# Count stage of a graph kernel: two-input compares, 128-column operands, and PSUM accumulators grouped in pairs

## The chip, the cores and the metric

The kernel runs on one core of a Trainium2 chip, as one launch. The metric is device time in microseconds (us) of a whole launch, lower is better. Three runs of the kernel before gave 2707.4, 2709.84 and 5465.59 us; their median is 2709.84 us. The profiled execution took 2711.62 us.

## The reference

Four graph layers in a row (a three-layer single-head GAT, a two-layer GCN, a relational GAT with four heads, an attention layer with FFN) work on one graph of 3125 nodes and 103,125 edges, 128 features per node, each followed by a residual and a layer norm. All of them use the edges only through sums over edges grouped by destination:

```
edge_index = jnp.stack([src, dst])                      # dst is sorted, edge_type_3 is 0, 1 or 2
out = jax.ops.segment_sum(msg, dst, num_segments=N)     # messages of edges added per destination
mask = jnp.concatenate([edge_type == r, jnp.ones((N,), dtype=bool)])   # third layer: relation r, and self loops
x = _layernorm(x + layer(x, edges, weights))            # four times
```

## The kernel before

The kernel first turns the edge list into dense count matrices, how many edges go from source s to destination d, for each of the three relations (`counts`) and in all (`counts_all`), and all layers then multiply by these. This case is about the stage that makes them, `count_edges`; the rest of the kernel is as it was.

**Tiling.** The 3125 nodes are 25 rows of P = 125. A destination is one of NG = 625 groups of DG = 5 destinations. The loop over i (25 iterations) takes 125 destinations, that is 25 groups b. A group's counts are a 125 x 375 matrix: source within its row by (relation, source row, destination within the group), 3 x 25 x 5 = 375 columns (GW; GE is 376, one more to keep it even). `prepare` has gathered, for every group, a window of WIN = 2 chunks of 125 edges that holds all edges of the group, one edge per partition: `window_lo` (source within its row) and `window_col` (column).

**One group.** DVE makes one-hot matrices by comparing an iota with these keys. For `lo1` (128 wide, both chunks, 1280 elements per partition) it does five groups in one compare of two tensors, L334. For `col1` (376 wide) it makes one compare with a per-partition scalar for each chunk, L339, ten for five groups. PE multiplies them, two matmuls of 375 columns added in one PSUM bank (L384). ACT copies the bank, 125 x 375, to the f16 tile `stage` (L438), where a group's columns become 75 runs of 5 elements: the destination is the innermost dimension of a row of 128.

**Sums over relations.** After each group b of `ADDED` = (3, 8, 13, 18, 23), PE adds the three relations of 25 destinations that are already in `stage` with six identity matmuls into two more banks (`add_up`, L370, called "the sums" below): sums number n = 0 after b = 3 (for the last 25 destinations of the iteration before), n = 1 after b = 8, and so on. Sums n wait (L367) until ACT has moved the result of sums n - 1 out of these two banks. ACT moves it to the tile `total` with two instructions (`move_total`, L427), which stand in its program after the copy of group b + 1, that is after b = 4, 9, 14, 19 and 24.

**What orders it.** The engines run their own programs in order and meet in counting semaphores: `hot` (one-hots of a group ready), `counted` (a group's matmuls done), `taken` (a group copied to `stage`), `summed` and `moved` (sums made, moved). Five banks hold groups (bank b % 5), two the sums. DVE may be at most five groups ahead of PE. POOL adds the self loops to `stage` and `total` (L322, four instructions per iteration, once the next iteration's n = 0 is moved), then the SP queue stores both, four DMAs of 800 KB (L453, L455). `stage` has three slots, `total` two. The branch for edges that do not fit the windows (`v.Else`, `pe.Else`) is not taken here.

Of the kernel before, what the change touches and what calls it, by code (L numbers as in the profile page):

```python
# [11 lines left out]
F32 = mybir.dt.float32  # L12
# [57 lines left out]
def prepare(nc, K, S):  # L70
# [7 lines left out]
    with ExitStack() as ctx:  # L78
# [20 lines left out]
        si = sb("si", [P, NG], I32)  # L99
        order = sb("order", [P, NG], F16)  # L100
        ki = sb("ki", [P, GE], I32)
        pi = sb("pi", [P, PAD, 2], I32)
        wt = sb("wt", [D, 6, D], F32)
        a = sb("a", [D, 6, 8], F32)
        m = sb("relm", [128, 2], F32)
# [6 lines left out]
        with nc.Block() as block:  # L112
# [27 lines left out]
            @block.gpsimd  # L140
            def _(pool):
                pool.iota(si[:], [[1, P], [P, DG]], channel_multiplier=0).then_inc(iotas, 1)
                pool.memset(K.ident[:], 0.0).then_inc(cleared, 1)
                pool.memset(K.ident16[:], 0.0).then_inc(cleared, 1)
                pool.memset(K.zeros[:], 0.0).then_inc(made, 1)
                pool.wait_ge(cleared, 2)
                for mat in (K.ident, K.ident16):
                    pool.affine_select(out=mat[:], in_=mat[:], compare_op=ALU.not_equal, fill=1.0, base=0,
                                       pattern=[[-1, 128]], channel_multiplier=1).then_inc(made, 1)
                pool.iota(gi[:], [[P, DG]], channel_multiplier=1).then_inc(iotas, 1)  # L150
                pool.iota(ti[:], [[GW, NG]], channel_multiplier=0).then_inc(iotas, 1)
                pool.iota(ki[:], [[1, GE]], channel_multiplier=0).then_inc(iotas, 1)
                pool.iota(pi[:], [[1, PAD], [0, 2]], channel_multiplier=0).then_inc(iotas, 1)
# [137 lines left out]
def count_edges(nc, K, S):  # L291
# [7 lines left out]
    STEPS = NCH // SLOTS  # L299
    HALVES = ((0, 13), (13, NB))  # L300
    ADDED = (3, 8, 13, 18, 23)

    with ExitStack() as ctx:
        sb = lambda name, shape, dt: ctx.enter_context(nc.sbuf_tensor(name, shape, dt))
        lo1 = sb("lo1", [P, P // DG, PAD, WIN], BF16)
        col1 = sb("col1", [P, SLOTS, GE], BF16)
        stage, total = K.stage, K.total
        lo_wide = lo1[:].rearrange("p s l w -> p (s l w)")[:, 0:SLOTS * PAD].rearrange("p (s l) -> p s l", l=PAD)
        (hot, counted, taken, summed, stored, diag, wide_hot, wide_used, moved) = (
# [2 lines left out]
        with nc.Block() as block:  # L312
# [12 lines left out]
            def _(v):  # L325
                wide = v.value_load(K.wide[0:1, 0:1], min_val=0, max_val=1)
                with v.If(wide < 1):
                    with v.Fori(0, NB) as i:
                        for b in range(P // DG):

                            v.wait_ge(counted, i * (P // DG) + b + 1)
                            if b % OHS == 0:

                                v.tensor_tensor(  # L334
                                    lo1[:, b:b + OHS], K.iota_pair[:].unsqueeze(1).to_broadcast([P, OHS, PAD, WIN]),
                                    K.window_lo[:, bass.ds(i * (P // DG) + b, OHS)].unsqueeze(2)
                                    .to_broadcast([P, OHS, PAD, WIN]), ALU.is_equal)
# [19 lines left out]

            @block.tensor
            def _(pe):
                pe.sem_inc(counted, OHS)  # L360
                pe.sem_inc(moved, 1)
                def add_up(i, n, own=True):

                    slot, q = (i % STAGES, n - 1) if own else ((i + STAGES - 1) % STAGES, 4)
                    pe.wait_ge(taken, i * (P // DG) + 5 * n + OHS)

                    pe.wait_ge(moved, 5 * i + n + 1)  # L367
                    for half, (h0, h1) in enumerate(HALVES):
                        for r in range(R):
                            ins = pe.matmul(K.ps[0:P, OHS + half, 0:(h1 - h0) * NB], K.ident16[0:P, 0:P],  # L370
                                            stage[0:P, bass.ds(slot, 1), r, h0:h1, bass.ds(25 * q, 25)]
                                            .rearrange("p a h d -> p (a h) d"), start=(r == 0), stop=(r == R - 1))
                    ins.then_inc(summed, 1)

                wide = pe.value_load(K.wide[0:1, 0:1], min_val=0, max_val=1)
                with pe.If(wide < 1):
                    with pe.Fori(0, NB) as i:
                        for b in range(P // DG):
                            s = b % OHS
                            pe.wait_ge(hot, i * (P // DG) + b + 1)  # L380
# [8 lines left out]
                with pe.Else():  # L389
                    pe.sem_inc(wide_used, 1)  # L390

                    def five_groups(i):
                        for s in range(OHS):

                            pe.wait_ge(taken, i * OHS + s + 1)
                            pe.matmul(K.ps[:, s, :], K.zeros[0:P, 0:128], K.zeros[0:P], start=True, stop=True)
                            with pe.Fori(0, STEPS) as c:
                                pe.wait_ge(wide_hot, i * (OHS * STEPS) + s * STEPS + c + 1)
                                for w in range(SLOTS):
                                    ins = pe.matmul(K.ps[0:P, s, 0:GW], lo_wide[:, w, 0:P], col1[:, w, 0:GW],  # L400
                                                    start=False, stop=False, skip_group_check=True)
                                ins.then_inc(wide_used, 1)

                            pe.matmul(K.ps[:, s, 0:128], K.zeros[0:P, 0:128], K.zeros[0:P, 0:128], start=False, stop=False,
                                      skip_group_check=True).then_inc(counted, 1)

                    with pe.Fori(0, NB) as i:
                        add_up(i, 0, own=False)
                        with pe.Fori(0, 4) as q:
                            five_groups(i * 5 + q)  # L410
                            add_up(i, q + 1)
                        five_groups(i * 5 + 4)

                add_up(NB, 0, own=False)

            @block.scalar
            def _(act):
                act.sem_inc(taken, OHS)

                def move_total(i, n):  # L420
                    act.wait_ge(summed, 5 * i + n + 1)
# [2 lines left out]
                        act.wait_ge(stored, 64 * i + 64 * (STAGES - 1))  # L424
                    slot, q = (i % 2, n - 1) if n else ((i + 1) % 2, 4)
                    for half, (h0, h1) in enumerate(HALVES):
                        ins = act.activation(total[0:P, bass.ds(slot, 1), h0:h1, 25 * q:25 * q + 25]  # L427
                                             .rearrange("p a h d -> p (a h) d"),
                                             K.ps[0:P, OHS + half, 0:(h1 - h0) * NB].rearrange("p (h d) -> p h d", d=NB),
                                             ACT.Copy)  # L430
                    ins.then_inc(moved, 1)

                with act.Fori(0, NB) as i:
                    act.wait_ge(stored, 64 * i + 64)
                    for b in range(P // DG):
                        act.wait_ge(counted, i * (P // DG) + b + 1 + OHS)
                        dst = stage[0:P, bass.ds(i % STAGES, 1), :, :, DG * b:DG * (b + 1)]
                        act.activation(dst.rearrange("p a r h d -> p (a r h) d"),  # L438
                                       K.ps[0:P, b % OHS, 0:GW].rearrange("p (x d) -> p x d", d=DG),
                                       ACT.Copy).then_inc(taken, 1)  # L440
# [1037 lines left out]
def build(nc, args, out):  # L1478
# [5 lines left out]
    with ExitStack() as ctx:  # L1484
# [25 lines left out]
        with nc.cleanup_on_exit():  # L1510
            with ExitStack() as c2:
# [4 lines left out]
                K.iota_pair = sb2("iota_pair", [P, PAD, WIN], F16)  # L1516
# [159 lines left out]
```

## Time and profile before

| | us |
|---|---|
| median of three runs | 2709.84 |
| profiled execution | 2711.62 |
| its span, first to last instruction | 2709.8 |
| count stage, first compare to last move of a total | 58.4 to 463.2 |
| one iteration of the stage, from the fourth on | 15.7 |

Of the whole span PE is busy 78%, DVE 79%, ACT 69%, POOL 3%. These are means over many stages. The count stage is some 405 us of it, and its numbers are read from windows inside it. In an answer of the trace on the order of time a row gives start and length in us, engine, line, operation, tiles and shapes and the number of merged instructions, and in brackets how long the engine had been idle before it and what ended that. Instructions of one engine overlap a little, so what an engine needs for one is the distance from start to start and not the duration; a length of n merged ones is n - 1 distances and one duration.

### The profile page before, as it was taken

The numbers are of one execution on the slowest core, as the hardware profiler recorded it, in microseconds if no ns is written. First come the engines' busy times: TensorE is split into PE (matmuls) and PEld (weight loads), VectorE is DVE, ScalarE is ACT, GpSimd is POOL, SyncE is SP. The second block draws the span as 40 slices with busy tenths as digits, with TensorE's granted clock in tenths as the row PEclk, the third lists the DMA queues.
The fourth block names the chain that finished last, engine by engine and source line by source line (L and its number), as shares of the span: only waits on it lengthen the run. The fifth ranks groups of instructions, "written<-read, shape, count | busy, mean of one in ns | idle before, by whom it ended". The sixth has DMA issues, their size and how long they took to land. (4 is left out here: it accounts for less than half of the span.)

```text
span 2709.8 us, 90541 instructions
## 1 busy us (share of the span) xinstructions
PE 2126.6 (78%) x34148; PEld 1879.1 (69%) x34148; DVE 2149.4 (79%) x4334; ACT 1869.8 (69%) x3038; POOL 85.4 (3%) x137
## 2 busy tenths in 40 slices
PE   3999997698599699494957999489995898766636
PEld 3655554598598598493957899389994898756624
DVE  6999997688787788606068999799988999949963
ACT  5999997666766765302049999599987999645522
POOL 1111111000000000000000000000000000000000
PEclk8999998799799799697988899799997999878868
DMA  3355455342342342171723331233303333034100
GB/s 100 147 224 210 193 220 216 108 143 78 99 152 77 108 143 77 61 242 61 242 72 92 92 105 52 81 95 107 102 28 110 98 95 107 3 110 133 60 0 24
DMA packets 182326, 302.60 MB, mean 112 GB/s; under 512 B 6476, under 2 KB 158927, under 8 KB 182058
## 3 DMA queue, kind: packets, MB, share of 16 engines
q1 hardware_dynamic: 181273, 297.57, 33.4%
q8 instruction: 208, 3.41, 0.6%
q0 software_dynamic: 800, 1.26, 0.2%
q14 instruction: 45, 0.37, 0.0%
HBM read 214.26 MB, written 84.54 MB: 110 GB/s over the span
## 5 line engine op out<-in xcount | busy, mean ns | idle before, releaser
L438 ACT ACTIVATE stage<-ps 125x375 f32 x625 | 314.0, 603 | 39.3 <-PE ps L384 34.9
L339 DVE TENSOR_SCALAR col<-iota_col,window_col 125x376 bf16<-125x376 f16 x1250 | 311.4, 327 | 4.4 <-PE ps L384 4.4
L384 PE MATMUL ps<-col,lo 125*125 125x375 bf16 x1250 | 290.9, 345 | 17.8 <-DVE col L339 17.5
L1007 ACT ACTIVATE r1amsk<-r1ad,r1thr 125x640 f16 x360 | 260.0, 815 | 2.5 <-DVE r1asel L1029 2.4
L1007 ACT ACTIVATE r2amsk<-r2ad,r2thr 125x640 f16 x360 | 259.7, 817 | 0.1
L1007 ACT ACTIVATE r0amsk<-r0ad,r0thr 125x640 f16 x360 | 259.6, 814 | 0.1
L1080 PE MATMUL ps<-r1mv,r1asel 125*128 125x66 f16 x5000 | 243.8, 196 | 9.8 <-issue 8.5
L1080 PE MATMUL ps<-r2mv,r2asel 125*128 125x66 f16 x5000 | 243.0, 196 | 5.3 <-issue 4.8
L1080 PE MATMUL ps<-r0mv,r0asel 125*128 125x66 f16 x5000 | 244.7, 197 | 0.3 <-DVE r0asel L1029 0.3
L384 PEld LDWEIGHTS ps<-col,lo 125*125 125x125 bf16 x1250 | 137.0, 139 | 145.0 <-DVE col L339 142.0
L1080 PEld LDWEIGHTS ps<-r1mv,r1asel 125*128 125x128 f16 x5000 | 227.0, 100 | 13.9 <-issue 9.1
L1080 PEld LDWEIGHTS ps<-r2mv,r2asel 125*128 125x128 f16 x5000 | 227.1, 100 | 7.9 <-issue 5.1
L1080 PEld LDWEIGHTS ps<-r0mv,r0asel 125*128 125x128 f16 x5000 | 229.2, 100 | 2.0 <-DVE r0asel L1029 0.4
L1084 PE MATMUL ps<-r0mv,r0ct 125*128 125x132 f16 x1250 | 181.2, 229 | 5.4 <-issue 5.4
L1084 PE MATMUL ps<-r1mv,r1ct 125*128 125x132 f16 x1250 | 180.3, 228 | 0.0
L1084 PE MATMUL ps<-r2mv,r2ct 125*128 125x132 f16 x1250 | 180.2, 228 | 0.0
L1225 PE MATMUL ps<-parts,ct 125*128 125x128 f16 x2500 | 150.4, 222 | 36.1 <-DVEq L1234 33.3
L1225 PEld LDWEIGHTS ps<-parts,ct 125*128 125x128 f16 x2500 | 143.2, 99 | 43.3 <-DVEq L1234 33.7
L949 PE MATMUL ps<-g0mv,g0asel 125*128 125x130 f16 x2500 | 147.9, 220 | 0.0
L949 PE MATMUL ps<-g2mv,g2asel 125*128 125x130 f16 x2500 | 147.3, 220 | 0.0
L949 PE MATMUL ps<-g1mv,g1asel 125*128 125x130 f16 x2500 | 147.0, 219 | 0.0
L949 PEld LDWEIGHTS ps<-g0mv,g0asel 125*128 125x128 f16 x2500 | 145.7, 97 | 0.6
(540 smaller groups left out, 4500.2 us busy)
## 6 DMA issues: line engine op xcount, KB each, us to landing
counts<-stage SPq DMA_DIRECT2D x75, 800.0 KB, 4.8
ct<-counts_all SPq DMA_DIRECT2D x75, 800.0 KB, 4.7
counts_all<-total SPq DMA_DIRECT2D x25, 800.0 KB, 7.3
g0ct<-counts_all SPq DMA_DIRECT2D x25, 800.0 KB, 4.6
g1ct<-counts_all SPq DMA_DIRECT2D x25, 800.0 KB, 4.7
g2ct<-counts_all SPq DMA_DIRECT2D x25, 800.0 KB, 4.6
r0ct<-counts SPq DMA_DIRECT2D x25, 800.0 KB, 4.7
r1ct<-counts SPq DMA_DIRECT2D x25, 800.0 KB, 6.3
```

The source lines that it names most:

```text
L339: ins = v.tensor_scalar(col1[:, b % OHS * WIN + w], K.iota_col[:], K.window_col[:, bass.ds(i * (P // DG) + b, 1), w], None, ALU.is_equal)
L384: ins = pe.matmul(K.ps[0:P, s, 0:GW], lo1[:, b, 0:P, w], col1[:, s * WIN + w, 0:GW], start=(w == 0), stop=(w == WIN - 1))
L438: act.activation(dst.rearrange("p a r h d -> p (a r h) d"), K.ps[0:P, b % OHS, 0:GW].rearrange("p (x d) -> p x d", d=DG), ACT.Copy).then_i ...
L949: ins = pe.matmul(K.ps[:, b, a * F:(a + 1) * F], sel[:, s % 5, a, b], T.mv[:, s, (2 * p + a) * F:(2 * p + a + 1) * F], start=False, stop=F ...
L1007: act.activation(msk[:, s % 5, n], ad[:, bass.ds(g % 2, 1), h] .rearrange("p a (b d) -> p (a b) d", d=PAD), ACT.Sigmoid, bias=T.thr[:, 1, ...
L1080: pe.matmul(K.ps[:, b, 2 * h * F:2 * (h + 1) * F], sel[:, s % 5, h, b], vs[:, (h * 2 + p) * 2 * F:(h * 2 + p + 1) * 2 * F], start=False, s ...
L1084: ins = pe.matmul(K.ps[:, b, 0:2 * HF].rearrange("p (h a f) -> p h a f", h=H, a=2)[:, :, 1], ct[0:P, s // 5, b, s % 5], vs[:, (4 + p) * HF ...
L1225: ins = pe.matmul(K.ps[:, b, 0:D], ct[0:P, s // 5, b, s % 5], parts[:, s, p], start=(s == 0 and p == 0), stop=(s == NB - 1 and p == 1))
```

## The change

- **Column one-hots.** They are made like `lo1`, by a compare of two tensors, for two groups and then for three, both chunks at once, into `col2`: [3 buffers, 5 groups, 376, 2 chunks], chunk innermost. So the matmul reads its moving operand with a step of two elements. `window_col` is f16 instead of f32 for that, `iota_pair` is 376 long instead of 128, and DVE waits once per five groups.
- **128 columns.** The stationary operands of L384 and L370 are 128 wide instead of 125, and so are the PSUM outputs and the copies.
- **Pairs.** Groups are taken in 13 pairs p (the last is group 24 alone). A pair has two neighbouring banks of six, in turns of three; the sums have banks 6 and 7. ACT copies a pair with one instruction of 2 x 375. PE waits for a free pair of banks before each pair's first group.
- **Place of the moves.** `move_total` stands after pairs 2, 5, 7, 10 and 12 for n = 0 to 4, so after the copy of groups 5, 11, 15, 21 and 24. `ADDED` is as it was.

```diff
-        pi = sb("pi", [P, PAD, 2], I32)
+        pi = sb("pi", [P, GE, 2], I32)
...
+    GROUPS = P // DG
+    SUMS = 6
+    PAIRS = [(b, min(b + 2, GROUPS)) for b in range(0, GROUPS, 2)]
+    BANK = [2 * (p % 3) for p in range(12)] + [2]
+    MOVED = {2: 0, 5: 1, 7: 2, 10: 3, 12: 4}
+    LAST = [max(p for p in range(len(PAIRS)) if BANK[p] == bank) for bank in (0, 2, 4)]
...
-        col1 = sb("col1", [P, SLOTS, GE], BF16)
+        col1 = sb("col1", [P, 30, GE], BF16)
+        col2 = col1[:].rearrange("p s c -> p (s c)").rearrange("p (a s c w) -> p a s c w", a=3, s=OHS, w=WIN)
...
-                        for b in range(P // DG):
-                            v.wait_ge(counted, i * (P // DG) + b + 1)
-                            if b % OHS == 0:
-                                v.tensor_tensor(
-                                    lo1[:, b:b + OHS], K.iota_pair[:].unsqueeze(1).to_broadcast([P, OHS, PAD, WIN]),
...
-                            for w in range(WIN):
-                                ins = v.tensor_scalar(
-                                    col1[:, b % OHS * WIN + w], K.iota_col[:],
-                                    K.window_col[:, bass.ds(i * (P // DG) + b, 1), w], None, ALU.is_equal)
-                            ins.then_inc(hot, 1)
+                        for n in range(GROUPS // OHS):
+                            v.wait_ge(counted, i * GROUPS + (5, 10, 10, 15, 20)[n])
+                            v.tensor_tensor(
+                                lo1[:, OHS * n:OHS * n + OHS], K.iota_pair[:, 0:PAD].unsqueeze(1).to_broadcast([P, OHS, PAD, WIN]),
...
+                            for s0, s1 in ((0, 2), (2, OHS)):
+                                v.tensor_tensor(
+                                    col2[:, n % 3, s0:s1], K.iota_pair[:].unsqueeze(1).to_broadcast([P, s1 - s0, GE, WIN]),
+                                    K.window_col[:, bass.ds(i * GROUPS + OHS * n + s0, s1 - s0)].unsqueeze(2)
+                                    .to_broadcast([P, s1 - s0, GE, WIN]), ALU.is_equal).then_inc(hot, s1 - s0)
...
+                def bank_free(i, b):
+                    p = b // 2
+                    earlier = [q for q in range(p) if BANK[q] == BANK[p]]
+                    if earlier:
+                        pe.wait_ge(taken, i * GROUPS + PAIRS[earlier[-1]][1] + GROUPS)
+                    else:
+                        pe.wait_ge(taken, i * GROUPS + PAIRS[LAST[BANK[p] // 2]][1])
...
-                            pe.wait_ge(taken, i * (P // DG) + b + 1)
+                            if b % 2 == 0:
+                                bank_free(i, b)
                             for w in range(WIN):
-                                ins = pe.matmul(K.ps[0:P, s, 0:GW], lo1[:, b, 0:P, w], col1[:, s * WIN + w, 0:GW],
+                                ins = pe.matmul(K.ps[:, BANK[b // 2] + b % 2, 0:GW], lo1[:, b, :, w],
+                                                col2[:, b // OHS % 3, b % OHS, 0:GW, w],
...
-                    for b in range(P // DG):
-                        act.wait_ge(counted, i * (P // DG) + b + 1 + OHS)
-                        dst = stage[0:P, bass.ds(i % STAGES, 1), :, :, DG * b:DG * (b + 1)]
...
-                        if b - 1 in ADDED:
-                            move_total(i, ADDED.index(b - 1))
+                    for p, (b0, b1) in enumerate(PAIRS):
+                        act.wait_ge(counted, i * GROUPS + b1 + 2 * OHS)
+                        dst = stage[:, bass.ds(i % STAGES, 1), :, :, DG * b0:DG * b1]
+                        act.activation(dst.rearrange("p a r h (s d) -> p s (a r h) d", d=DG),
+                                       K.ps[:, BANK[p]:BANK[p] + b1 - b0, 0:GW].rearrange("p s (x d) -> p s x d", d=DG),
+                                       ACT.Copy).then_inc(taken, b1 - b0)
+                        if p in MOVED:
+                            move_total(i, MOVED[p])
...
-                K.window_col = sb2("window_col", [P, NG, WIN], F32)
+                K.window_col = sb2("window_col", [P, NG, WIN], F16)
```

## Rows read from the trace of the kernel before

**Rows 1.** Busy time by window, one iteration: PE, PEld, DVE, ACT, POOL, clock, DMA
```profile
251.38:267.09 15.71, 15.18 (x82) 9.11 (x81) 15.71 (x57) 14.95 (x36) 2.10 (x4) 1.00 0.51 209
```
**Rows 2.** Who waited for whom, 62 to 455 us: total, times, longest
```profile
PEld ps L384 <- DVE col L339: 136.1, 456, 0.6
ACT stage L438 <- PE ps L384: 16.2, 26, 1.4
PE ps L370 <- ACT total L427: 4.3, 8, 2.6
```
**Rows 3.** Timeline of DVE from 267 us: compares of five groups
```profile
267.09 0.82 DVE L334 TENSOR_TENSOR lo<-iota_pair,window_lo 125x1280 bf16<-125x1280 f16 x1
267.82 2.36 DVE L339 TENSOR_SCALAR col<-iota_col,window_col 125x376 bf16<-125x376 f16 x10
```
**Rows 4.** Timeline from 257 us, POOL beside DVE
```profile
257.58 1.71 POOL L322 TENSOR_TENSOR stage<-stage,ident 125x125 f16 x3 [13.60 <-ACT total L427]
258.12 3.04 DVE L339 TENSOR_SCALAR col<-iota_col,window_col 125x376 bf16<-125x376 f16 x10
```
**Rows 5.** Timeline from 109 us, where PE was not held by DVE
```profile
108.69 1.75 PE L384 MATMUL ps<-col,lo 125*125 125x375 bf16 x10
109.29 0.67 ACT L438 ACTIVATE stage<-ps 125x375 f32 x1 [1.26 <-PE ps L384]
109.80 0.74 ACT L427 ACTIVATE total<-ps 125x325 f32 x2
110.68 1.04 PE L370 MATMUL ps<-stage,ident 125*125 x6 [0.24 <-ACT total L427]
111.56 1.16 PE L384 MATMUL ps<-col,lo 125*125 125x375 bf16 x5
```
**Rows 6.** Timeline of ACT from 263 us, instruction by instruction
```profile
263.10 0.44 ACT L427 ACTIVATE total<-ps 125x325 f32 x1
263.43 0.41 ACT L427 ACTIVATE total<-ps 125x300 f32 x1
263.73 0.51 ACT L438 ACTIVATE stage<-ps 125x375 f32 x1
264.10 0.52 ACT L438 ACTIVATE stage<-ps 125x375 f32 x1
264.48 0.70 ACT L438 ACTIVATE stage<-ps 125x375 f32 x1
264.97 0.54 ACT L438 ACTIVATE stage<-ps 125x375 f32 x1
```
**Rows 7.** Groups of instructions, 0 to 62 us (second number after the first bar: mean ns)
```profile
L258 ACT ACTIVATE stage<-zeros 128x28800 f16<-128x28800 bf16 x1 | 24.2, 24204 | 9.2 <-POOL zeros L145 9.2
L258 ACT ACTIVATE total<-zeros 128x6400 f16<-128x6400 bf16 x1 | 5.5, 5519 | 0.0
```
**Rows 8.** Busy time by window, the third iteration
```profile
89.27:110.06 20.79, 17.16 (x81) 11.65 (x80) 16.74 (x57) 14.60 (x34) 4.12 (x8) 0.84 0.76 310
```
**Rows 9.** Timeline from 101 us, in the third iteration
```profile
101.53 0.77 ACT L427 ACTIVATE total<-ps 125x325 f32 x2 [3.38 <-DMA counts_all<-total]
102.44 0.53 PE L370 MATMUL ps<-stage,ident 125*125 x1 [2.58 <-ACT total L427]
```
**Rows 10.** Groups of instructions, whole span
```profile
L1080 PEld LDWEIGHTS ps<-r0mv,r0asel 125*128 125x128 f16 x5000 | 229.2, 100 | 2.0 <-DVE r0asel L1029 0.4
L384 PEld LDWEIGHTS ps<-col,lo 125*125 125x125 bf16 x1250 | 137.0, 139 | 145.0 <-DVE col L339 142.0
L370 PEld LDWEIGHTS ps<-stage,ident 125*125 125x125 f16 x756 | 99.1, 136 | 27.4 <-issue 15.6
L917 DVE TENSOR_TENSOR g1asel<-g1ct,g1asel 125x640 f16<-125x640 f16 x125 | 61.5, 492 | 4.3
```
**Rows 11.** Timeline of the preparation, the instructions that grow
```profile
33.78 0.29 DVE L198 CAST iota_pair<-pi 125x256 f16<-125x256 int32 x1
37.24 1.53 POOL L158 DMA_INDIRECT above<-edge_keys,rows_of  x1 [22.05 <-DVE rows_of L210]
```

More of the change, by code:

```diff
@@ L152, in _ @@
                 pool.iota(ki[:], [[1, GE]], channel_multiplier=0).then_inc(iotas, 1)
-                pool.iota(pi[:], [[1, PAD], [0, 2]], channel_multiplier=0).then_inc(iotas, 1)
+                pool.iota(pi[:], [[1, GE], [0, 2]], channel_multiplier=0).then_inc(iotas, 1)
                 pool.wait_ge(rows_ready, 1)
@@ L328, in _ @@
                     with v.Fori(0, NB) as i:
[L329 to L342 removed]
+                        for n in range(GROUPS // OHS):
+                            v.wait_ge(counted, i * GROUPS + (5, 10, 10, 15, 20)[n])
+                            v.tensor_tensor(
+                                lo1[:, OHS * n:OHS * n + OHS], K.iota_pair[:, 0:PAD].unsqueeze(1).to_broadcast([P, OHS, PAD, WIN]),
+                                K.window_lo[:, bass.ds(i * GROUPS + OHS * n, OHS)].unsqueeze(2)
+                                .to_broadcast([P, OHS, PAD, WIN]), ALU.is_equal)
+                            for s0, s1 in ((0, 2), (2, OHS)):
+                                v.tensor_tensor(
+                                    col2[:, n % 3, s0:s1], K.iota_pair[:].unsqueeze(1).to_broadcast([P, s1 - s0, GE, WIN]),
+                                    K.window_col[:, bass.ds(i * GROUPS + OHS * n + s0, s1 - s0)].unsqueeze(2)
+                                    .to_broadcast([P, s1 - s0, GE, WIN]), ALU.is_equal).then_inc(hot, s1 - s0)
                 with v.Else():
@@ L359, in _ @@
             def _(pe):
-                pe.sem_inc(counted, OHS)
+                pe.sem_inc(counted, 2 * OHS)
                 pe.sem_inc(moved, 1)
+                def bank_free(i, b):
[5 more added lines that the diff above has]
+                        pe.wait_ge(taken, i * GROUPS + PAIRS[LAST[BANK[p] // 2]][1])
                 def add_up(i, n, own=True):
                     slot, q = (i % STAGES, n - 1) if own else ((i + STAGES - 1) % STAGES, 4)
-                    pe.wait_ge(taken, i * (P // DG) + 5 * n + OHS)
+                    pe.wait_ge(taken, i * GROUPS + 5 * n + GROUPS)
                     pe.wait_ge(moved, 5 * i + n + 1)
@@ L369, in add_up @@
                         for r in range(R):
-                            ins = pe.matmul(K.ps[0:P, OHS + half, 0:(h1 - h0) * NB], K.ident16[0:P, 0:P],
-                                            stage[0:P, bass.ds(slot, 1), r, h0:h1, bass.ds(25 * q, 25)]
+                            ins = pe.matmul(K.ps[:, SUMS + half, 0:(h1 - h0) * NB], K.ident16[:],
+                                            stage[:, bass.ds(slot, 1), r, h0:h1, bass.ds(25 * q, 25)]
                                             .rearrange("p a h d -> p (a h) d"), start=(r == 0), stop=(r == R - 1))
@@ L377, in _ @@
                     with pe.Fori(0, NB) as i:
-                        for b in range(P // DG):
-                            s = b % OHS
-                            pe.wait_ge(hot, i * (P // DG) + b + 1)
-                            pe.wait_ge(taken, i * (P // DG) + b + 1)
+                        for b in range(GROUPS):
+                            pe.wait_ge(hot, i * GROUPS + b + 1)
+                            if b % 2 == 0:
+                                bank_free(i, b)
                             for w in range(WIN):
-                                ins = pe.matmul(K.ps[0:P, s, 0:GW], lo1[:, b, 0:P, w], col1[:, s * WIN + w, 0:GW],
+                                ins = pe.matmul(K.ps[:, BANK[b // 2] + b % 2, 0:GW], lo1[:, b, :, w],
+                                                col2[:, b // OHS % 3, b % OHS, 0:GW, w],
                                                 start=(w == 0), stop=(w == WIN - 1))
@@ L390, in _ @@
                     pe.sem_inc(wide_used, 1)
[L392 to L405, printed above, removed]
@@ L407, in _, with one_group @@
-                    with pe.Fori(0, NB) as i:
[L408 to L412, printed above, removed]
+                    def one_group(i, b):
+                        bank = BANK[b // 2] + b % 2
+                        bank_free(i, b)
+                        pe.matmul(K.ps[:, bank, :], K.zeros[0:P, 0:128], K.zeros[0:P], start=True, stop=True)
+                        with pe.Fori(0, STEPS) as c:
+                            pe.wait_ge(wide_hot, i * (GROUPS * STEPS) + b * STEPS + c + 1)
+                            for w in range(SLOTS):
+                                ins = pe.matmul(K.ps[:, bank, 0:GW], lo_wide[:, w], col1[:, w, 0:GW],
+                                                start=False, stop=False, skip_group_check=True)
+                            ins.then_inc(wide_used, 1)
+                        pe.matmul(K.ps[:, bank, 0:128], K.zeros[0:P, 0:128], K.zeros[0:P, 0:128], start=False, stop=False,
+                                  skip_group_check=True).then_inc(counted, 1)
@@ L414, in _ @@
+                    with pe.Fori(0, NB) as i:
+                        for b in range(GROUPS):
+                            one_group(i, b)
+                            if b in ADDED:
+                                add_up(i, ADDED.index(b), own=(b != ADDED[0]))
                 add_up(NB, 0, own=False)
@@ L417, in _ @@
             def _(act):
-                act.sem_inc(taken, OHS)
+                act.sem_inc(taken, GROUPS)
                 def move_total(i, n):
@@ L426, in move_total @@
                     for half, (h0, h1) in enumerate(HALVES):
-                        ins = act.activation(total[0:P, bass.ds(slot, 1), h0:h1, 25 * q:25 * q + 25]
+                        ins = act.activation(total[:, bass.ds(slot, 1), h0:h1, 25 * q:25 * q + 25]
                                              .rearrange("p a h d -> p (a h) d"),
-                                             K.ps[0:P, OHS + half, 0:(h1 - h0) * NB].rearrange("p (h d) -> p h d", d=NB),
+                                             K.ps[:, SUMS + half, 0:(h1 - h0) * NB].rearrange("p (h d) -> p h d", d=NB),
                                              ACT.Copy)
@@ L434, in _ @@
                     act.wait_ge(stored, 64 * i + 64)
-                    for b in range(P // DG):
-                        act.wait_ge(counted, i * (P // DG) + b + 1 + OHS)
-                        dst = stage[0:P, bass.ds(i % STAGES, 1), :, :, DG * b:DG * (b + 1)]
-                        act.activation(dst.rearrange("p a r h d -> p (a r h) d"),
-                                       K.ps[0:P, b % OHS, 0:GW].rearrange("p (x d) -> p x d", d=DG),
-                                       ACT.Copy).then_inc(taken, 1)
-                        if b - 1 in ADDED:
-                            move_total(i, ADDED.index(b - 1))
+                    for p, (b0, b1) in enumerate(PAIRS):
[6 more added lines that the diff above has]
+                            move_total(i, MOVED[p])
                 move_total(NB, 0)
@@ L1515, in build @@
                 K.iota_col = sb2("iota_col", [P, GE], F16)
-                K.iota_pair = sb2("iota_pair", [P, PAD, WIN], F16)
+                K.iota_pair = sb2("iota_pair", [P, GE, WIN], F16)
                 K.window_lo = sb2("window_lo", [P, NG, WIN], F16)
-                K.window_col = sb2("window_col", [P, NG, WIN], F32)
+                K.window_col = sb2("window_col", [P, NG, WIN], F16)
                 K.wide = sb2("wide", [1, 1], I32)
```

## The prediction

> **What bounds the stage now.** I read first the busy time of single iterations, then the waits, then the timeline. An iteration takes 15.71 us and DVE is busy for all of it [rows 1]; PE waited for `col` 456 times [rows 2], with 625 groups in the whole stage. So DVE sets the pace. ACT is close behind, 14.95 us busy. Five groups cost DVE 0.73 us for `lo` (start to start) and 2.27 for the ten column compares, 3.00 in all [rows 3]. Once per iteration POOL's four additions come between: the ten compares then last 3.04 instead of 2.36, +0.68 [rows 4]. 5 x 3.00 + 0.68 = 15.7, the measured period.
>
> PE alone would be faster: matmuls start every 0.16 us ((1.75 - 0.32) / 9, with 0.32 for the last one's own duration), six sums hold it 1.04 at most, 0.84 without the start-up [rows 5]. 50 x 0.16 + 5 x 0.84 = 12.2 us. What it does when DVE doesn't hold it is seen once, and the prediction rests on it [rows 5]. The copy of the group begun at 108.69 starts 0.60 later (two matmuls 0.48, then 0.13 until ACT is off); the total is moved by 110.54; 0.14 later the sums start, and PE had idled 0.24. That is the loop sums, copy, move of a total, next sums. It is hidden today because four groups lie between the copy that precedes the move and the next sums, and at DVE's pace these take 4 x 0.45.
>
> **DVE's part.** `lo` has 1280 elements, lasts 0.82 and costs 0.73 start to start [rows 3]; one of the same kind with 640 lasts 0.49 [rows 10]. So 0.33 / 640 = 0.52 ns per element, and 0.07 fixed. The new compares have the same kind, dtypes and broadcast: 2 x 752 elements 0.85, 3 x 752 elements 1.24. Five groups: 0.73 + 0.85 + 1.24 = 2.82. With POOL's four interruptions, which I leave at 0.68 (they already wait for a two-input compare at 257.58, rows 4), an iteration would be 14.8 us: -0.9, if DVE stayed the bound.
>
> **ACT's part.** A copy of 375 costs 0.37 to 0.38 or 0.49 start to start [rows 6]. Which one goes by group. The 75 runs of 5 f16 start at byte 10b of their row; the four copies shown are groups 15 to 18, and the long one is 17, whose run, bytes 170 to 180, crosses a multiple of 16. So do 12 of the 25. A pair has the same runs, so its cost is the two singles less one fixed part. From the two fills, (24204 - 5519) / 22400 = 0.834 ns per element [rows 7]; 375 elements are 0.313, so the fixed part of a start-to-start 0.375 is 0.06. A pair with one long copy: 0.375 + 0.495 - 0.06 = 0.81. Ends: 0.87 (nothing saved) and 0.63 (750 elements at 0.834 and nothing else). The Trainium skill (ScalarE: Activation LUTs, What ACT_TABLE_LOAD costs) has back-to-back ACTIVATEs at a fixed 93 ns beyond the elements; by it the pair is 0.78 and the period below 0.2 us shorter, and the sum doesn't use it. Moving a total stays 0.33 + 0.41 = 0.74 [rows 6].
>
> **The new order, on the path.** Sums n still wait for total n - 1 to be moved. That move now stands after groups 5, 11, 15, 21, 24 instead of 4, 9, 14, 19, 24. Before sums 1, 2, 3, 4, 0 PE has only 3, 2, 3, 2, 4 groups left to do, and ACT copies a pair only when its second group is done. From the start of one set of sums to the start of the next, with 0.88 for the sums after a wait (110.68 to 111.56, rows 5), 0.32 per full group, 0.48 for a last one, 0.13 to ACT and 0.13 back:
> - 1 to 2: group 9 must end before pair (8, 9) is copied, then pair (10, 11), then the total: 0.88 + 0.48 + 0.13 + 0.81 + 0.81 + 0.74 + 0.13 = 3.98. PE's own work there is 0.84 + 10 x 0.16 = 2.4, so it idles 1.5.
> - 2 to 3: pair (14, 15) needs two groups after the sums: 0.88 + 0.32 + 0.48 + 0.13 + 0.81 + 0.74 + 0.13 = 3.49.
> - 3 to 4, as the first: 3.98.
> - 4 to 0: group 24 alone is copied, 0.88 + 0.48 + 0.13 + 0.51 + 0.13 = 2.13; only then are the banks free for pair (2, 3), since the last pair uses the same ones; two groups and the start-up, 0.70. 2.83.
> - 0 to 1: pair (4, 5), as 2 to 3 less the start-up, 3.45.
>
> Sum 17.7 us per iteration, against DVE's 14.8, ACT's own 13.3 (13 x 0.375 + 12 x 0.495 - 12 x 0.06 + 5 x 0.62) and PE's 12.2: nobody is full, they take turns. With a pair at 0.87 it is 18.1, at 0.63 16.6 (six pairs are on the loop).
>
> So (17.73 - 15.71) x 25 = +51. Against it, the third iteration loses less. Today ACT waits 3.38 us in it for the first store of a total and PE stops for 2.6 [rows 9]; the iteration has a mean clock of 0.84, so a third of it at 1.2 GHz, and takes 20.8 us, 5 more than the others [rows 8]. At 17.7 us per iteration that move comes at about 102, when the store has landed: -5. Sum +46. Later stores have room, the DMA engines are busy 0.51 x 15.7 = 8 us per iteration [rows 1]. At the ends +55 and +19.
>
> **At nothing.** The stationary loads should fall from 139 towards 100 ns [rows 10], but they lie under matmuls of 160. POOL's iota is three times as long under a wait of 22 us. The cast of `iota_pair` (0.29) grows by some 0.3 us beside sums that PE still has to finish [rows 11], the first group's one-hots come 0.4 later; if no cover holds, +0.7 in all. POOL's additions each wait for a longer compare, up to 4.4 us instead of 2.1; the store that follows has that slack, without it the total's double buffer would hold ACT.
>
> **Forecast.** 2711.6 + 46 = 2758 in the profiled execution, 2756 against the median of 2709.84, since that execution was 1.8 above it. Its own range is 2729 to 2767. 2%, about what a measurement of this kernel tells from no change, is 54 us: 2764. Chance 0.63, of which 0.17 above 2764.
>
> **Rivals.**
> - DVE stays the bound: I misread the loop, or ACT is much quicker with a pair. 14.8 us, 25 x -0.9 = -22: 2688. For it: ACT was busy 14.95 of 15.71 and sheds twelve fixed parts. Against: the loop falls to 15.7 only if a pair costs 0.46, below its elements' 0.63. Decides from there on. 0.20, of which 0.03 faster by over 2%.
> - The moving operand reads at half rate. Today 375 neighbouring bf16 take 0.16, which is 2.4 GHz with one column per cycle; with every second element, twice the bytes are passed over. No row shows a moving operand with a step; a stationary one with the same step (`lo`) loads in 139 ns beside 136 without [rows 10], which speaks against. Matmuls at 0.31: the segments become 4.75, 4.13, 4.75, 4.0, 4.13, sum 21.8, +6.1 x 25 - 5: 2859. The Trainium skill, SBUF — State Buffer, gives this port 2 bytes per lane and cycle (A bandwidth-pool intuition that's wrong), which would do this, but also says (Door 1) that two hits per 16-byte line give full rate, which a step of 4 bytes has. No run shows either. 0.10.
> - The wide compares fall to one element per cycle, twice the 0.52 ns: 3760 x 1.04 ns + 0.13 + 0.73 = 4.78 per five groups, 24.6 per iteration, 2930. Against: `lo` has the same form. 0.03.
> - PE's clock falls in the idle stretches. It is at 1.00 over whole iterations [rows 1] and fell only in the iteration with the stop of 2.6 us [rows 8, 9]; here PE would stop 1.5 us at most and work 60% of its idlest segment. At half clock throughout, matmuls as in the rival above and sums longer too, up to 2950. 0.04.
>
> **Sum of chances.** Faster by over 2%: 0.03. Slower by over 2%: 0.17 + 0.10 + 0.03 + 0.04 = 0.34. Within: 0.63. The range takes the forecast's 2729 to 2767 and reaches down to the first rival: 2686 to 2773.
>
> **What would show it.** Right: iterations of 17.7 us; DVE idle about 3 us in each, ended by L384; PE idle 1.5 before the second and fourth sums and 1 before the first and third, ended by ACT's total; a pair's copy about 0.81 start to start; matmuls still 0.16 apart. Wrong: DVE busy throughout, matmuls 0.31 apart, column compares of 1.6 and 2.4 us, a clock below 1.00 in the stage, or a pair far from 0.81.

## The result, and the profile after

The changed kernel takes 2762.55 us, median of four runs (2755.81 to 2769.8), beside 2708.62 for the kernel before in the same comparison: ratio 1.020, 95% interval 1.019 to 1.021. One of the four runs of the kernel before took 5465.59 us, twice its usual time; without it that median is 2707.4. The changed kernel's profiled execution is the quickest of its four, 2755.81, with a span of 2754.0 and a mean clock of 0.904.

One steady iteration of the stage by the window view (columns as in [rows 1]):

```profile
270.13:288.35 18.22, 13.50 (x82) 7.39 (x80) 15.25 (x16) 14.71 (x24) 4.39 (x5) 1.00 0.44 180
```

18.22 us, against 15.71 in [rows 1]. No engine fills it: DVE was busy for all of its iteration before and now lacks 3 us, and ACT's busy time has hardly moved. The clock stays at 1.00. The waits from 62 to 500 us, which are most of the stage, to be held against [rows 2]:

```profile
PE ps L385 <- ACT total L441: 111.6, 95, 1.4
ACT stage L452 <- PE ps L399: 104.9, 121, 19.6
DVE lo L339 <- PE ps L399: 75.3, 47, 4.2
PE ps L399 <- DVE col L344: 5.3, 1, 5.3
```

PE waited for `col` 456 times; now once. Its new wait is for the move of a total, 95 times in the 119 sums of that window, and ACT waits for PE nearly as long. One iteration of PE by the timeline, five sums and the matmuls between them:

```profile
273.95 1.01 PE L385 MATMUL ps<-stage,ident 128*128 x6 [1.40 <-ACT total L441]
274.82 1.82 PE L399 MATMUL ps<-col,lo 125*128 125x375 bf16 x10
277.57 1.00 PE L385 MATMUL ps<-stage,ident 128*128 x6 [0.93 <-ACT total L441]
...
281.65 1.00 PE L385 MATMUL ps<-stage,ident 128*128 x6 [1.42 <-ACT total L441]
...
284.46 1.00 PE L385 MATMUL ps<-stage,ident 128*128 x6
...
288.11 1.00 PE L385 MATMUL ps<-stage,ident 128*128 x6 [0.98 <-ACT total L441]
```

The idle times alternate, 1.4 and 0.95. The same stretch on ACT shows why: two pair copies stand ahead of the total where PE waits 1.4, one where it waits 0.95.

```profile
271.35 1.86 ACT L452 ACTIVATE stage<-ps 128x750 f32 x2 [0.77 <-PE ps L399]
273.05 0.76 ACT L441 ACTIVATE total<-ps 128x325 f32 x2
...
275.77 1.02 ACT L452 ACTIVATE stage<-ps 128x750 f32 x1 [1.08 <-PE ps L399]
276.68 0.75 ACT L441 ACTIVATE total<-ps 128x325 f32 x2
```

Taken one by one, the two copies of the first row are:

```profile
271.35 1.02 ACT L452 ACTIVATE stage<-ps 128x750 f32 x1 [0.77 <-PE ps L399]
272.21 1.00 ACT L452 ACTIVATE stage<-ps 128x750 f32 x1
```

And DVE, which stops twice per iteration because PE is behind:

```profile
275.08 2.17 DVE L344 TENSOR_TENSOR col<-iota_pair,window_col 125x1504 bf16<-125x1504 f16 x2
279.06 0.83 DVE L339 TENSOR_TENSOR lo<-iota_pair,window_lo 125x1280 bf16<-125x1280 f16 x1 [1.81 <-PE ps L399]
279.80 2.18 DVE L344 TENSOR_TENSOR col<-iota_pair,window_col 125x1504 bf16<-125x1504 f16 x2
283.14 0.82 DVE L339 TENSOR_TENSOR lo<-iota_pair,window_lo 125x1280 bf16<-125x1280 f16 x1 [1.16 <-PE ps L399]
```

The first compare comes at 60.09 (before 58.38) and the last move of a total ends at 525.62 (463.15): the stage is 60.8 us longer. The profiled execution is only 44 longer, because everything behind the stage took 18 us less than in the profiled execution of before. The stages of the third layer show it, before (first fence) and after (second), by the window view:

```profile
1399.10:1722.40 323.30, 264.31 (x6339) 256.91 (x6339) 294.61 (x359) 290.11 (x411) 3.14 (x2) 0.90 0.29 86
1722.40:2045.50 323.10, 264.43 (x6339) 255.09 (x6340) 290.12 (x355) 290.54 (x411) 3.16 (x3) 0.90 0.30 86
```

```profile
1460.35:1778.08 317.73, 263.64 (x6339) 255.66 (x6339) 294.27 (x359) 290.12 (x411) 3.14 (x2) 0.90 0.30 88
1778.08:2094.72 316.64, 262.00 (x6339) 254.49 (x6339) 289.97 (x355) 290.04 (x411) 3.14 (x2) 0.92 0.29 88
```

The same instructions with the same busy times on DVE and ACT, 6 us shorter each. The profiled executions of experiments 1, 3, 6 and 9 below give back 10 to 18 us behind the stage too, that of experiment 2 nothing. The granted clock differs in one of the two windows only. Over everything behind the stage it is 0.89 against 0.88, so part of the 18 us may be the clock; but in experiment 6 it is 0.88 there as before, and that part is 10 us shorter all the same. Why stays open.

### The profile page after: what moved, and what is told of

Its sections match the earlier page's. It is cut to its first block and busy times, and to the rows that moved or that the text cites. A ratio compares the mean times of both kernels' runs of the same rounds, so it can differ in the third digit from the quotient of the medians.

```text
span 2754.0 us, 86841 instructions
## 1 busy us (share of the span) xinstructions
PE 2082.4 (76%) x34148; PEld 1826.1 (66%) x34148; DVE 2135.2 (78%) x3334; ACT 1863.3 (68%) x2738; POOL 145.2 (5%) x137
## 5 line engine op out<-in xcount | busy, mean ns | idle before, releaser
L452 ACT ACTIVATE stage<-ps 128x750 f32 (+1 forms) x325 | 306.0, 982 | 109.1 <-PE ps L399 109.1
L344 DVE TENSOR_TENSOR col<-iota_pair,window_col 125x1504 bf16<-125x1504 f16 x250 | 281.7, 1167 | 0.0
L399 PE MATMUL ps<-col,lo 125*128 125x375 bf16 x1250 | 235.3, 330 | 5.4 <-DVE col L344 5.3
L385 PE MATMUL ps<-stage,ident 128*128 x756 | 128.0, 305 | 121.0 <-ACT total L441 117.8
L385 PEld LDWEIGHTS ps<-stage,ident 128*128 128x128 f16 x756 | 72.7, 96 | 188.8 <-issue 168.4
L399 PEld LDWEIGHTS ps<-col,lo 125*128 125x128 bf16 x1250 | 113.8, 97 | 92.7 <-issue 16.7
L339 DVE TENSOR_TENSOR lo<-iota_pair,window_lo 125x1280 bf16<-125x1280 f16 x125 | 112.1, 897 | 78.1 <-PE ps L399 76.5
```

The lines of the kernel that those rows point to most:

```text
L339: v.tensor_tensor(lo1[:, OHS * n:OHS * n + OHS], K.iota_pair[:, 0:PAD].unsqueeze(1).to_broadcast([P, OHS, PAD, WIN]), K.window_lo[:, bass. ...
L344: v.tensor_tensor(col2[:, n % 3, s0:s1], K.iota_pair[:].unsqueeze(1).to_broadcast([P, s1 - s0, GE, WIN]), K.window_col[:, bass.ds(i * GROU ...
L385: ins = pe.matmul(K.ps[:, SUMS + half, 0:(h1 - h0) * NB], K.ident16[:], stage[:, bass.ds(slot, 1), r, h0:h1, bass.ds(25 * q, 25)] .rearran ...
L399: ins = pe.matmul(K.ps[:, BANK[b // 2] + b % 2, 0:GW], lo1[:, b, :, w], col2[:, b // OHS % 3, b % OHS, 0:GW, w], start=(w == 0), stop=(w = ...
L452: act.activation(dst.rearrange("p a r h (s d) -> p s (a r h) d", d=DG), K.ps[:, BANK[p]:BANK[p] + b1 - b0, 0:GW].rearrange("p s (x d) -> p ...
```

## The experiments

Each ran beside the kernel before on the same chip. "Steady" is the mean period of an iteration from the fourth on in the profile. The kernel before has 15.70, the changed one 18.22. An interval in brackets is that of the ratio at 95%.

**1. Only the place of the moves goes back**, as early as pairs allow.

```diff
-    MOVED = {2: 0, 5: 1, 7: 2, 10: 3, 12: 4}
+    MOVED = {1: 0, 4: 1, 6: 2, 9: 3, 12: 4}
```

> The changed kernel with one line altered: the totals are moved after pairs 1, 4, 6, 9, 12 (groups 3, 9, 13, 19, 24) instead of 2, 5, 7, 10, 12. Theory M: from 18.2 us to 15.6 to 16.0 per iteration, because between the sums and the next sums only one pair copy is left on the loop; about 2709 in all, ratio 1.00. Rival B (the pairs themselves cost it: PE waits for a free pair of banks and ACT for a pair's second group, wherever the moves stand): 17.5 or more per iteration, ratio above 1.015.

Measured: 2705.99, ratio 0.997 (0.995 to 0.999), steady 15.98.

```profile
243.20:259.18 15.98, 13.54 (x81) 7.33 (x80) 15.25 (x16) 14.30 (x24) 4.40 (x5) 1.00 0.50 205
```

The whole loss hangs on this one line: pairs, compares and columns are all still there.

**2. Only the place of the moves changes**, in the kernel before: the copies stay single, DVE stays as it was.

```diff
+    MOVED = {5: 0, 11: 1, 15: 2, 21: 3, 24: 4}
...
-                        if b - 1 in ADDED:
-                            move_total(i, ADDED.index(b - 1))
+                        if b in MOVED:
+                            move_total(i, MOVED[b])
```

> The kernel before with the moves of totals placed as in the change, after groups 5, 11, 15, 21, 24, and nothing else: single copies, single banks, old compares. Theory M: part of the loss comes with this alone, 16.6 us per iteration instead of 15.7 and a third iteration that loses less, about 2728, ratio 1.007. Rival B: no change, ratio 1.00.

Measured: 2741.08, ratio 1.0097 (1.006 to 1.013), steady 17.0. Half of the 2.5 us per iteration comes with the place alone, a little more than I had expected (16.6). The rest comes with the pairs; by the timeline they make the copy ahead of the move twice as long and let it begin one group later. PE's wait for the move, from 62 to 490 us:

```profile
PE ps L371 <- ACT total L428: 88.6, 99, 1.9
```

**3. The changed kernel with the old compares**: DVE's work as before, moving operand without a step.

```diff
...
-                                                col2[:, b // OHS % 3, b % OHS, 0:GW, w],
+                                                col1[:, b // OHS % 3 * 2 * OHS + b % OHS * WIN + w, 0:GW],
...
```

> The changed kernel with the old column compares (ten with a per-partition scalar for five groups, f32 keys) into three buffers, so that the moving operand is contiguous again; pairs, banks, 128 columns and moves as in the change. Theory M: DVE isn't the bound there, so nothing changes, 18.2 us per iteration, ratio 1.02 as the change. Rival C: back towards 15.7 us, ratio 1.00.

Measured: 2760.24, ratio 1.017 (1.014 to 1.020), steady 18.1. The new compares buy nothing in the changed order, and the stepped operand costs nothing there.

**4. The new compares alone**, without pairs, places or columns (the compares of the diff, DVE up to ten groups ahead, three buffers of `col2`).

> The kernel before with the change's compares alone: column one-hots by two-input compares in three buffers, the matmul's moving operand with a step of two; five single banks, single copies of 375 and moves of the total after groups 4, 9, 14, 19, 24 as before, 125 columns. Theory M (the loss is the loop sums, pair copy, move of a total, next sums): here that loop is short and DVE sets the pace with 5 x 2.83 + 0.69 = 14.8 us per iteration, so 25 x -0.9 = -22 us, +2 for the preparation: about 2689, ratio 0.993. Rival C (the compares or the stepped operand cost more than they save): iterations of 15.7 us or longer, ratio 1.00 to 1.02.

Measured: 2797.86, ratio 1.032 (1.028 to 1.035). A clear miss. When it runs, PE makes sums every 2.9 us, as expected. But in seven of the 25 iterations POOL is held, and after each ACT stops for 16 us, waiting for the store of a total: from the fourth on, iterations take 15.1, 14.2 and 32.2 us in turn, 20.5 in the mean. The timeline of POOL where one such stop begins, of DVE beside it, and of ACT behind it:

```profile
255.16 22.62 POOL L324 TENSOR_TENSOR stage<-stage,ident 125x125 f16 x3 [9.51 <-ACT total L427]
277.74 0.42 POOL L324 TENSOR_TENSOR total<-total,ident 125x125 f16 x1
...
257.58 2.17 DVE L339 TENSOR_TENSOR col<-iota_pair,window_col 125x1504 bf16<-125x1504 f16 x2
259.68 0.81 DVE L334 TENSOR_TENSOR lo<-iota_pair,window_lo 125x1280 bf16<-125x1280 f16 x1
260.41 2.17 DVE L339 TENSOR_TENSOR col<-iota_pair,window_col 125x1504 bf16<-125x1504 f16 x2
...
287.91 0.77 ACT L427 ACTIVATE total<-ps 125x325 f32 x2 [16.17 <-DMA counts_all<-total]
```

POOL's first addition of 125 x 125 lasts 21.9 us, the next ones 0.42: it begins when DVE's compares run without a gap and gets through only when DVE has run out of work, 22 compares later (the last of them ends at 276.74, the addition at 277.02). DVE's own instructions aren't lengthened meanwhile (0.81 and 2.17 for two, as without POOL). The store waits for the addition, the double buffer of `total` for the store, ACT for the buffer. The Trainium skill (SBUF — State Buffer, Who interferes with whom) says that a DVE instruction with two SBUF inputs contends with a GpSimd instruction that reads SBUF, and that the one issued first makes the other block. The trace agrees in kind; here the block outlasted not one instruction of DVE but 22.

**5. The 128 columns alone**, in the kernel before.

```diff
...
-                                ins = pe.matmul(K.ps[0:P, s, 0:GW], lo1[:, b, 0:P, w], col1[:, s * WIN + w, 0:GW],
+                                ins = pe.matmul(K.ps[:, s, 0:GW], lo1[:, b, :, w], col1[:, s * WIN + w, 0:GW],
...
```

> The kernel before with 128-column operands and copies over 128 partitions, and nothing else of the change. Every theory expects no change: DVE still sets the pace at 15.7 us per iteration, the stationary loads fall from 139 to about 97 ns and lie under matmuls 160 ns apart. 2714, ratio 1.000 +- 0.002. If the ratio is above 1.003, a part of the change that was costed at nothing costs something.

Measured: 2712.51, ratio 0.9996 (0.997 to 1.002), steady 15.70. Nothing, as expected. Its runs spread from 2705 to 2723, and those of the kernel before beside it from 2705 to 2725. The profiled one, 2721, shows where such a run can come from: POOL's very first addition is held even by the old compares, for 13.4 us, and in the third iteration ACT waits 14.7 us for the store of a total, where it was 3.38 before [rows 9].

```profile
88.13 14.14 POOL L322 TENSOR_TENSOR stage<-stage,ident 125x125 f16 x3 [33.05 <-issue]
```

**6. Compares and columns, POOL's additions left out** (the self loops aren't counted).

> The compares and the 128 columns alone, and POOL's additions are left out (the self loops are not counted), so that POOL issues nothing beside DVE. Theory L (lock-out: DVE's two-input compares, issued back to back, can keep POOL's addition from beginning, and that is the whole of the 16 us stops): no stop at all, iterations at 5 x 2.82 = 14.1 us if DVE is the bound or up to 14.6 if ACT's own 14.5 is; 25 x -1.1 to -1.6, plus 2 of preparation: 2676 to 2688, ratio 0.986 to 0.990. Rival S (the stops come from something else in the new order of DVE, its ten groups of lead or the store of a total): the stops of 16 us stay in two of three iterations, 2798, ratio 1.03.

Measured: 2669.48, ratio 0.984 (0.980 to 0.988), steady 14.48, no stop. The stops of experiment 4 are POOL's. That the median is below the expected range while 14.48 is inside it has two reasons: the third iteration, 20.79 us before, takes 14.52, a gain of 5 us that the expectation had left out, and the part behind the stage is 10 us shorter in this profiled execution.

**7. The compares alone, POOL's additions begun at a fixed place** in DVE's stream.

```diff
...
                     pool.wait_ge(moved, 5 * i + 7)
+                    pool.wait_ge(hot, 25 * i + 37)
...
```

> The compares alone, as in the run that took 2798, but POOL's four additions now also wait until DVE has finished the compare for groups 10 and 11, so that the first one starts about 0.1 us into a compare of three groups. That is where it stood 0.08 us after a compare's start in eight iterations of that run, and there it got in each time (1,524 ns). Theory L with a phase (whether POOL gets in is settled by where in DVE's compare it starts): all 25 take some 5 us, no stop, iterations at 14.6 to 14.9 us, 2690 to 2698, ratio 0.992 to 0.995. Rival (chance, or the number of compares in a row decides): some iterations still stop for 16 us, 2720 to 2800.

Measured: 2805.58, ratio 1.033 (1.029 to 1.038), steady 20.5 like experiment 4. The first additions begin 0.46 us into the compare and not the 0.1 that was meant (in experiment 4, all eight that began at 0.08 got in). The theory of the phase fell all the same, since one place gives both outcomes. Two first additions that both start 0.46 us after the same compare of DVE began:

```profile
243.15 3.19 POOL L321 TENSOR_TENSOR stage<-stage,ident 125x125 f16 x3 [22.91 <-DVE col L343]
...
258.22 21.72 POOL L321 TENSOR_TENSOR stage<-stage,ident 125x125 f16 x3 [10.41 <-DVE col L343]
```

One gets in between two compares and from then on POOL and DVE take turns; the other is shut out. Nothing in the trace that I found separates them in advance.

**8. The compares alone, self loops added by DVE**, after its third batch of the next iteration; POOL does nothing.

```diff
...
+                            if n == 2 and not first:
+                                self_loops(i - 1)
...
```

> The compares alone, and DVE makes the four additions of self loops itself, after its third batch of the next iteration; POOL does nothing in the stage. An addition of 125 f16 should take DVE 0.13 (0.07 fixed and 125 x 0.52 ns), four 0.5. Theory L: no stop, 14.1 + 0.5 = 14.6 us, or ACT's own 14.5 and what it waits: 2688 to 2695, ratio 0.991 to 0.994. Rival S: the stops of 16 us stay, 2798. If DVE has to wait for the move of total 0 at that place, an idle DVE is seen ahead of the additions and the iteration is longer by it.

Measured: 2684.07, ratio 0.989 (0.985 to 0.993), steady 14.69 and no stop, as expected; the median is 4 us below the expected range. The four additions on DVE, which POOL needs 1.7 us for undisturbed:

```profile
260.93 0.56 DVE L322 TENSOR_TENSOR stage<-stage,ident 125x125 f16 x3
261.33 0.29 DVE L322 TENSOR_TENSOR total<-total,ident 125x125 f16 x1
261.47 0.88 DVE L330 TENSOR_TENSOR lo<-iota_pair,window_lo 125x1280 bf16<-125x1280 f16 x1
```

From 260.93 to 261.47, 0.54 us in all.

**9. The whole change, self loops added by DVE** (the same edit).

> The whole change, with the four additions of self loops made by DVE after its third batch and none by POOL. Theory P (the change's loss is the loop of sums, pair copy and move of a total, and POOL has no part in it: in its trace two of POOL's additions were locked out for 6.5 us, but nothing waited for them): DVE has 3 us of idle time per iteration in which its four additions of 0.14 lie, iterations stay at 18.1 to 18.2 us, 2757 to 2763, ratio 1.016 to 1.020. Rival L (contention of POOL and DVE is part of the loss): DVE's batches without POOL save 0.7 us per iteration on the path, 17.5 us, 2745, ratio 1.012 or less.

Measured: 2759.11, ratio 1.019 (1.017 to 1.020), steady 18.22.

```profile
PE ps L398 <- ACT total L454: 113.3, 96, 1.4
ACT stage L465 <- PE ps L412: 104.9, 122, 19.5
```

The waits are those of the changed kernel. POOL has no part in its loss, although in the changed kernel too two of its first additions were shut out, until DVE's next idle time:

```profile
397.62 7.30 POOL L329 TENSOR_TENSOR stage<-stage,ident 125x125 f16 x3 [13.81 <-ACT total L441]
```

**10. The kernel before, self loops added by DVE.**

> The kernel before with its old compares, and the self loops added by DVE instead of POOL: which part of the gain of the run that took 2684 is the compares, which POOL's going. DVE is the bound: 5 x 3.00 + 4 x 0.14 = 15.56 us per iteration instead of 15.70, 25 x -0.14 = -3.5. If the stop in the third iteration, whose store comes after POOL's additions, is owed to POOL's late first additions, up to 5 more goes: 2705 to 2710, ratio 0.997 to 0.9985. Rival (going without POOL is worth most of the 28 us, since a two-input operation of POOL slows the old compares too): below 2700.

Measured: 2699.88, ratio 0.997 (0.996 to 0.998), steady 15.57, and the third iteration takes 15.57 too instead of 20.79. The ratio is where it was expected (the kernel before was at 2707.41 in this comparison, 6 below the level from which I had worked out the time, which is why the rival's "below 2700" is just met; the period of 15.57 and the third iteration are the theory's). In the kernel before POOL's first addition started only at 88.74, the first store was issued at 91.92; here it is issued at 84.48, and ACT never waits for it. On POOL and the SP queue before (first fence), and on the SP queue here (second):

```profile
88.74 2.43 POOL L322 TENSOR_TENSOR stage<-stage,ident 125x125 f16 x3 [34.75 <-issue]
91.92 2.17 SPq L453 DMA_DIRECT2D counts<-stage  x3
```

```profile
84.48 2.17 SPq L466 DMA_DIRECT2D counts<-stage  x3
```

The total that POOL waits for had been moved by 80.45; what keeps it for the 8.3 us more no row shows (in the changed kernel it is 7.5). The eight runs lie within 4 us, the eleven of the kernel before beside them within 7.

**11. The candidate: compares, 128 columns, self loops on DVE**; copies single and moves where they were before.

> The candidate: the two-input compares and the 128 columns of the change, single copies and moves where they were before, and the self loops added by DVE. The columns alone gave 0.9996, so 14.7 us per iteration as without them, 2684, ratio 0.989 +- 0.002. DVE's need of 14.65 and ACT's of 14.5 are then nearly equal, and PE waits for both. If the wider loads and copies matter once DVE isn't far ahead of them, the ratio is off 0.989 by more than its interval.

Measured: 2682.54, ratio 0.990 (0.989 to 0.992).

```profile
250.50:265.19 14.69, 13.90 (x82) 7.16 (x81) 14.69 (x20) 14.52 (x36) 0.00 (x0) 1.00 0.55 223
```

It beats both kernels, by 1.0% and, over the two comparisons, some 2.9%. Experiment 8 does so too and is within the uncertainty of it, so the columns remain worth nothing that can be measured. DVE is full again, with ACT close behind.

## Why the prediction was right, and where it was off

The forecast was 2756, the median is 2762.55: 2.0% where 1.7% had been forecast, inside the range and near the upper end of the forecast's own, 2767. By its steps:

- **What bounded the kernel.** DVE, as forecast: with four additions of its own, 0.54 us, in place of the 0.68 that POOL cost it, and nothing else (experiment 10), the period fell by 0.13.
- **The mechanism.** The loop sums, copy, move, next sums. Right, and shown from both sides: moves early in the changed kernel take the loss away (experiment 1), moves late in the kernel before bring half of it (experiment 2), and neither DVE's work (3) nor POOL's (9) matters. The spacings of the sums were forecast one by one:

| us, start to start | 1 to 2 | 2 to 3 | 3 to 4 | 4 to 0 | 0 to 1 |
|---|---|---|---|---|---|
| forecast | 3.98 | 3.49 | 3.98 | 2.83 | 3.45 |
| measured | 4.07 | 3.62 | 4.08 | 2.81 | 3.65 |

- **The size.** 18.22 instead of 17.7 per iteration, 12 us in the stage. The part of the loop that ACT has was mis-sized: from the start of one pair's copy to the sums behind its total it is 277.57 - 275.77 = 1.80, where 0.81 + 0.74 + 0.13 = 1.68 was put; with two pairs 273.95 - 271.35 = 2.60 for 2.49. Nearly all of it is the pair's copy. Start to start the two pairs are 0.86 and 0.84 (271.35, 272.21, 273.05), the single one 0.91 (276.68 - 275.77), and the six on the loop come to 0.87 in the mean of the iterations from 110 to 480 us, the upper end that the prediction kept: 6 x 0.06 = 0.4 of the 0.5 us, about 0.02 per total moved being the rest. The fixed part that merging two copies should have saved, 0.06, isn't there: a pair right behind another instruction takes 0.84 to 0.88, one that ACT had waited for 0.85 to 0.91, and two singles 0.87.
- **The third iteration.** 18.24, like its neighbours, as forecast: the stop went. Its cause was put too simply, "the first store": it was POOL's late first additions that held that store (experiments 5 and 10). In the changed kernel they are as late, but its longer iterations leave the store the time.
- **The sum.** +46 was forecast for the stage and 60.8 came: 12 of the difference from the period, 3 from the first two iterations and from what follows the last. Ahead of the stage came 1.7 more (first compare 60.09 for 58.38), where +0.7 had been the most; but that time varies as much in kernels whose preparation is the old one (59.35 in experiment 2, 59.47 in experiment 5). The profiled execution still came out at +44 = 60.8 + 1.7 - 18.3, because what follows the stage took 18 us less. These are errors that cancel, and that the time came so close is luck; by the medians the change costs 54. Two slips in the working change nothing: ACT's own 13.3 adds up to 13.2, and of the forecast's own range the lower end counts from 2709.84 and the upper from 2711.6.
- **DVE's part.** A batch of five groups takes 2.84 (283.14 to 285.98, start to start), forecast 2.82; beside POOL 3.53 (270.59 to 274.12), so POOL costs the same 0.7 as before, as assumed.
- **POOL's additions, "up to 4.4 us instead of 2.1".** 270.08 to 274.48 is 4.4, but the bound was no bound: the four took 7.7 us twice (397.62 to 405.30). In the changed kernel the store's slack covers that. In experiment 4 the same term, 23.0, decides everything. The prediction's rival "DVE stays the bound: 2688" had this hole: with DVE full of two-input compares, POOL's share isn't 0.68. That case as it really is takes 2798, so a price of "waits for a longer compare" should have had an end for "doesn't get in at all".
- **The rivals.** The stepped moving operand runs at full rate: 277.57 + 0.84 = 278.41, ten matmuls in 1.82, (1.82 - 0.33) / 9 = 0.166 each. Of the two passages of the Trainium skill (SBUF — State Buffer), the one on 16-byte lines (Door 1) agrees; the other, read as I read it in the rival, does not. Wide compares at one element per cycle, and a lower clock in the stage: neither came.

## What to carry to other kernels

Before moving a step behind another on an in-order engine, write down who waits for it and count the work that lies between; grouping two copies lengthens the piece of work that stands in front of everything behind them, and saved at most 0.03 us here. Once engines take turns, making one of them faster is worth nothing (experiment 3), and the same edit is worth 0.6% where that engine is full (2682.54 in experiment 11 beside 2699.88 in experiment 10). Small POOL work beside a full DVE isn't small: move it to DVE (0.54 us) if a store or a buffer hangs on it.

## What the runs showed of the hardware that was not expected

- Two-input instructions of DVE without a gap can keep a POOL instruction waiting for 21.9 us, 22 of them in a row; it gets in when DVE idles. It happened in 7 of 25 iterations of experiments 4 and 7, in every third one; in 2 of 25 of the changed kernel; in none of experiment 1. The old stream, ten one-input compares for each two-input one, does it too: once for 13.4 us, past 48 instructions, and in most iterations of experiments 2 and 3 for a first addition of 1.6 and 2.0 us, past five and four. What decides between taking turns and being shut out stays open; the place in DVE's stream, to 0.01 us, does not.
- While they take turns, both pay: `lo` 1.05 instead of 0.82, POOL's additions 0.9 to 1.5 instead of 0.42.
- A stationary load of 128 columns lasts 97 ns where one of 125 lasted 139 [rows 10], and it made no difference to the time here.
